# The Nyquist bin's running sums in a holographic attention kernel: two products of three columns instead of five of one

## What is computed

```
x_k = ifft(unit(fft(k)) * unit(fft(v)))
s   = cumsum(x_k, over the tokens)
out = ifft(fft(s) * conj(unit(fft(q))))
```

## Time and profile before

| | us |
|---|---|
| three runs | 1918.32, 1919.68, 1920.07 |
| median | 1919.68 |
| the profiled execution | 1920.69 |
| its span in the profile | 1918.9 |
| PE busy | 1867.1 (97%) |
| PE weight loads busy | 1417.2 (74%) |
| VectorE busy | 1500.1 (78%) |
| ScalarE busy | 1118.4 (58%) |
| GpSimd busy | 946.1 (49%) |

### The profile page before, as it was taken

How to read it: one execution, slowest core, us unless ns; L and a number is a source line. 1 busy time by engine, 2 the same in 40 slices (tenths; PEclk the granted TensorE clock), 3 DMA queues, 4 the chain that set the end, 5 groups by cost and what they waited for, 6 DMA issues and landing times.

```text
span 1918.9 us, 40326 instructions
## 1 busy us (share of the span) xinstructions
PE 1867.1 (97%) x14680; PEld 1417.2 (74%) x14680; DVE 1500.1 (78%) x2874; ACT 1118.4 (58%) x2151; POOL 946.1 (49%) x736
## 2 busy tenths in 40 slices
PE   8599999999999999999999999999999999999978
PEld 6478777778777778877777877777877777887755
DVE  4878778877877877877877877787787787788783
ACT  5666565566555566556556656556656555655643
POOL 1254445564454565444555444556444556545450
PEclk9799999999999999999999999999999999999998
DMA  8022232222133222223222223222213322222212
GB/s 285 12 78 81 74 99 88 77 88 87 55 99 99 66 88 88 67 86 99 77 84 86 82 66 99 93 71 88 88 56 97 99 75 79 88 67 87 88 56 66
DMA packets 181784, 163.18 MB, mean 85 GB/s; under 512 B 140160, under 2 KB 140800, under 8 KB 181760
## 3 DMA queue, kind: packets, MB, share of 16 engines
q1 hardware_dynamic: 163328, 95.48, 16.8%
q0 software_dynamic: 18432, 67.38, 10.6%
HBM read 95.72 MB, written 16.78 MB: 59 GB/s over the span
## 4 chain that ended last, share of the span: by engine, by line
PE 93%; DVE 1%; DMA 0%; SPq 0%; ACT 0%; issue 0%; DVEq 0%; ACTq 0%
PE bank_l L531 31%; PE bank_l L591 30%; PE bank_p L481 24%; PE bank_l L541 3%; PE bank_i L481 2%; PE bank_i L552 1%; PE bank_i L561 0%; PE bank_i L562 0%; PE bank_i L560 0%; PE bank_i L559 0%; DMA arena<-xn_pair 0%; PE bank_i L558 0%; PE bank_i L571 0%; SPq L340 0%; DVE xn_pair L1127 0%
## 5 line engine op out<-in xcount | busy, mean ns | idle before, releaser
L531 PE MATMUL bank_l<-arena,win_mem 128*128 128x256 f16 x5376 | 626.1, 273 | 14.4 <-DMA arena<-xn_pair 14.4
L591 PE MATMUL bank_l<-wout_mem,arena 128*128 128x512 f16 x2688 | 590.6, 379 | 0.0
L531 PEld LDWEIGHTS bank_l<-arena,win_mem 128*128 128x128 f16 x5376 | 527.3, 99 | 76.5 <-DMA arena<-xn_pair 14.2
L481 PE MATMUL bank_p<-arena,wf_hi 128*128 128x256 f16 x3072 | 506.3, 273 | 2.7 <-ACT arena L742 2.7
L591 PEld LDWEIGHTS bank_l<-wout_mem,arena 128*128 128x128 f16 x2688 | 263.1, 98 | 303.4 <-DVE arena L1224 0.2
L481 PE MATMUL bank_p<-arena,wf_lo 128*128 128x256 f16 x1536 | 419.3, 273 | 0.0
L986 POOL TENSOR_TENSOR arena<-arena 128x512 f32<-128x512 f32 x96 | 121.7, 1268 | 570.2 <-ACT arena L751 570.2
L481 PEld LDWEIGHTS bank_p<-arena,wf_hi 128*128 128x128 f16 x3072 | 299.8, 98 | 37.7 <-ACT arena L742 3.0
L796 ACT ACTIVATE arena<-bank_l,bias_in,s_logit 128x256 f32<-128x256 f32 x448 | 229.6, 556 | 142.1 <-PE bank_l L541 141.6
L1224 DVE SCALAR_TENSOR_TENSOR arena<-arena,s_act 128x512 f16<-128x512 f32 (+1 forms) x256 | 195.5, 765 | 133.7 <-ACT arena L806 131.2
L1217 DVE TENSOR_SCALAR dec<-bank_l,thr,off 128x256 bf16<-128x256 f32 x256 | 135.8, 541 | 91.5 <-PE bank_l L531 88.8
(11 more groups left out here) (178 smaller groups left out, 2490.3 us busy)
## 6 DMA issues: line engine op xcount, KB each, us to landing
arena<-in_x SPq DMA_DIRECT2D x32, 512.0 KB, 3.5
arena<-arena SPq DMA_DIRECT2D x32, 512.0 KB, 2.9
out<-arena SPq DMA_DIRECT2D x64, 256.0 KB, 2.1
wout_mem<-in_w_in_t SPq DMA_DIRECT2D x1, 3584.0 KB, 15.4
arena<-in_w_out_t SPq DMA_DIRECT2D x1, 3584.0 KB, 14.2
arena<-xn_pair SPq DMA_TRANSPOSE x128, 2.7
arena<-in_leaf_rows,leaf_row POOLq DMA_INDIRECT x128, 5.5
win_mem<-in_wq SPq DMA_DIRECT2D x1, 1024.0 KB, 8.2
```

The costliest lines, as they stand in the source:

```text
L481: mm = pe.matmul(bank, a, b, start=(n == 0), stop=(n == len(pairs) - 1))
L531: mm = pe.matmul(bank_l[t % 4][:, c * T:(c + 1) * T], a[:, k, w:w + P], x2t[:, :, b, k, :], start=(c == 0 and k == 0 and m == 0), stop=((t ...
L591: mm = pe.matmul(bank_l[j][:, :], a[:, m, tok], w[:, m, :], start=(m == 0 and a is a_hi and w is wout_hi), stop=(m == DENSE - 1 and a is a ...
```

## The change

The tile `sp_kv` gets five columns, of which the third is set to zero once and never written again. VectorE writes the products of both groups to columns 0 and 1, the product of group 0 once more to column 3, and the sum of both to column 4. TensorE multiplies `upper` by columns 0 to 2 and adds `full` times columns 2 to 4, so that all three columns of `sp_sums` come of two matmuls.

```diff
-        sp_kv = sb("sp_kv", [P, J])
+        sp_kv = sb("sp_kv", [P, 2 * J + 1])
...
+        sp_bound = sem("sp_bound")
...
             def nyquist_sums(n):
 
                 pe.wait_ge(sp_kv_ready, n + 1)
-                pe.matmul(sp_sums[:, 0:1], upper, sp_kv[:, 0:1], start=True, stop=True)
-                pe.matmul(sp_sums[:, 1:2], upper, sp_kv[:, 1:2], start=True, stop=False)
-                pe.matmul(sp_sums[:, 1:2], full, sp_kv[:, 0:1], start=False, stop=True)
-                pe.matmul(sp_sums[:, 2:3], full, sp_kv[:, 0:1], start=True, stop=False)
-                pe.matmul(sp_sums[:, 2:3], full, sp_kv[:, 1:2], start=False, stop=True).then_inc(sp_sums_full, 1)
+                pe.matmul(sp_sums[:, 0:3], upper, sp_kv[:, 0:3], start=True, stop=False)
+                pe.matmul(sp_sums[:, 0:3], full, sp_kv[:, 2:5], start=False, stop=True).then_inc(sp_sums_full, 1)
...
             pool.memset(carry[:, :], 0.0)
+            pool.memset(sp_kv[:, :], 0.0)
             pool.memset(sp_carry[:, :], 0.0).then_inc(cleared, 1)
...
             def nyquist_bind(n):
 
                 dve.wait_ge(sp_hat_ready, n + 1)
-                dve.tensor_tensor(sp_kv[:, :], sp_hat[:, :, K], sp_hat[:, :, V], ALU.mult).then_inc(sp_kv_ready, 1)
+                dve.tensor_tensor(sp_kv[:, 0:2], sp_hat[:, :, K], sp_hat[:, :, V], ALU.mult)
+                dve.tensor_tensor(sp_kv[:, 3:4], sp_hat[:, 0, K:K + 1], sp_hat[:, 0, V:V + 1], ALU.mult).then_inc(sp_bound, 1)
+                dve.wait_ge(sp_bound, n + 1)
+                dve.tensor_tensor(sp_kv[:, 4:5], sp_kv[:, 0:1], sp_kv[:, 1:2], ALU.add).then_inc(sp_kv_ready, 1)
```

## The result

| | before | changed |
|---|---|---|
| first measurement, median us | 1919.9 (4 runs) | 1904.9 (1902.0 to 1905.4, 4 runs) |
| ratio, 95% interval | | 0.992 (0.9908 to 0.9932) |
| second measurement, another chip | 1920.3 (9 runs) | 1903.0 (1901.5 to 1904.6, 5 runs) |
| ratio, 95% interval | | 0.9912 (0.9899 to 0.9926) |
| profiled execution / its span | 1920.7 / 1918.9 | 1902.0 / 1899.9 |

A forecast was written before the change was run, and what follows sets the result against it. TensorE was taken to bound the steady blocks. -20.5 (sums) + 0.3 (start-up) + 1.2 (tree 7) = -19.0 us, giving 1900.7 us; own range 1898 to 1903, extended to 1907 for part of the collision.

The forecast's parts named there:

- Two matmuls for five: TensorE's Nyquist-bin sums in each steady block: 0.37 us for 1.04, saving 0.66 us, 20.5 us over 31 blocks.
- The rival by which columns set the price: TensorE's sums: six columns replace five and six 25 ns launches go, 4.7 us less in all, 1915 us; chance 0.02.
- the estimate by the rule of the Trainium skill: TensorE's sums: six fewer matmul records at 25 ns each would save 150 ns a block.
- VectorE's two operations: VectorE's products for the sums: two more operations and a wait, 0.26 us more a block, hidden in steady blocks.
- that idle time hides it: VectorE's 1.50 us of idle time in front of act_low 5 absorbs the added 0.26 us in steady blocks.
- The 0.3 us of the start-up: Start-up, where VectorE has no idle time before z_low: its added 0.26 us counts once.
- The wait at tree 7: TensorE waits for act_low 7, late behind POOL's unbinding products: 0.04 us a block, 1.2 us over 31 blocks.
- The play-through: Turns of VectorE's act_lows and POOL's products, act_lows issued 0.66 us earlier: act_low 7 ends only 0.19 us earlier.
- The load of x: Load of the next x ahead of the feed-forward transposes: their issue distance shrinks from 2.41 to 1.96 us, no added wait.
- With 1.96 I take zero: With 1.96 us between issuing the load of x and the first feed-forward transpose, TensorE has no added wait.
- the load of x collides: Rival: the load meets the feed-forward transposes, each block waits 0.4 us, 1913 us; chance 0.11.
- The slower rival: act_low 7 loses one more turn to POOL, tree 7 waits 1.7 us, blocks 1.0 us longer, 1951 us; chance 0.03.

The follow-up runs named there:

- the one-matmul kernel: Changed kernel with only the first of the two matmuls, the whole-group product left out of the computation: 1897.2 us, ratio 0.988 against the kernel before.
- `act_high` 7: Changed kernel with ScalarE's act_high 7 moved ahead of the next block's two high operations: 1899.4 us, ratio 0.9894 against the kernel before.

## Why the prediction was right or wrong

- **Two matmuls for five: right.** 0.66 us a block was said; PE's stream is shorter by 0.67 us (56.87 to 56.20 us where nothing else holds it), the three-column matmul takes 0.22 us where 0.225 was said. (The lower bound, 31 x 0.59, is 18.3 us and not 18.2, which changes nothing.) The rival by which columns set the price is out: one more matmul of three columns cost 0.22 us in the row, and one fewer as much in undisturbed blocks. With it falls, for this fp32 case, the estimate by the rule of the Trainium skill (TensorE: Matmul & The Clock Gate, section "Wait — 56ns, not 53.3ns?"), 0.15 us a block.
- **VectorE's two operations: right in size (0.26 us), wrong in effect.** The step "that idle time hides it" looked at VectorE alone. With the operations POOL's third and fourth descriptors and unbind also come 0.06 us later. By themselves they cost nothing that shows (ratio 1.0001); beside the saving the wait at tree 7 is 0.10 us instead of 0.04. The 0.3 us of the start-up are smaller than the scatter there, and no run shows them. Why POOL's descriptors come later was not tried.
- **The wait at tree 7: right in its mechanism, mis-sized.** 0.04 us was said, 0.09 measured: 2.5 us in all for 1.2. The play-through had act_low 7 end 11.21 us after the counts; it ends at 11.30, and 0.07 of that is POOL's later start. Its release was over-sized (0.06 us, not 0.10).
- **The load of x: this step failed.** "With 1.96 I take zero" took the distance of the two issues for the whole of the matter. The distance came out as forecast (1.94 us), but at it the transposes land up to 0.9 us later than before in some steps, and in one of them PE waited. Step 1 (1.05 us) and step 29 (1.14 us) wait as well, step 29 for 1.3 or 0.6 us in place of 0.4. The rival "the load of x collides" was thus true in three blocks of the first trace and in one of the second, and not in all. The wait in step 30, 0.5 or 1.05 us, was in no term and no rival: it has no load, and goes together with an instruction packet among its transposes. All in all it is 2.4 and 1.7 us in place of 0.4.
- **The sum.** From the waits, -20.6 (31 x 0.665) + 0.3 + 2.5 + 2.0 = -15.8 us, 1904.1 us from 1919.9; from the starts of the counts, 30 blocks are 14.6 us shorter in the first trace and 15.3 in the second, and the block before them adds 0.67. Measured: 1904.9 us, 15.0 less, and on another chip 1903.0, 17.3 less, of which the traces explain 16.0. The forecast's -19.0 misses the two mis-sized terms, 1.3 us at tree 7 and 1.3 to 2.0 at the transposes. The first median lies outside the forecast's own 1898 to 1903, the second at its end; what held both was the part to 1907 that it gave to the collision, and a part of the collision is what came.
- **The slower rival** never came: POOL doesn't pass VectorE twice. The turn can also fall the other way, which the one-matmul kernel shows.

## What to carry to other kernels

When the time saved lies ahead of a point from which other engines run on a time of their own, they become late by exactly what is saved: list what does not move with the saving (here POOL's chain behind its gather) and what it meets. Two engines that take turns, as VectorE and POOL here, can make a step of a whole operation out of a shift of tenths, so look for an operation issued just behind the other engine's start, and move it ahead by order, as `act_high` 7 here. Small operations that sit in one engine's idle time are free only as long as nobody else in the chain is due. And profile the changed kernel twice before a sum of small waits is explained: here it was 2.4 us once and 1.7 the next time.

## What the runs showed of the hardware that was not expected

An fp32 matmul with 128 x 128 weights costs 0.22 us of PE's time with one column as with three (rows of both, here and in the earlier trace rows), against 25 ns for an fp16 matmul of one column in a row of four. With two more VectorE operations of 0.15 us, on tiles of one column, the third of POOL's gather descriptors came 0.06 us later in most blocks, beside five matmuls as beside two. A transpose behind the load of 512 KB landed 2.75 to 3.8 us after its issue at distances of 1.8 to 2.1 us, from step to step and from execution to execution, and behind 256 KB within 2.80 us. The transposes of step 30 landed 3.5 to 4.5 us after their issue (one of the two at least) in the nine traces where a 16 KB instruction packet started 35.0 to 36.8 us after the counts, and within 2.82 us in the four where it started earlier. In step 28 the second gather descriptor starts about 1.9 us later than in other steps, in every kernel profiled here. That is the odd block; that the one makes the other was not tried, and the cause stays open.
